# Unmasked cross attention: row maxima over pieces of 512 columns, with the last 65 columns of four tiles in one bank

## The reference, cut to what matters

```python
q = _split_heads(query @ q_w + q_b, B)      # (1, 16, 2048, 16)
k = _split_heads(key @ k_w + k_b, B)        # (1, 16, 1601, 16)
v = _split_heads(value @ v_w + v_b, B)
scores = jnp.einsum('bhqd,bhkd->bhqk', q, k) * SCALE
attn = jax.nn.softmax(scores, axis=-1)
out = jnp.einsum('bhqk,bhkd->bhqd', attn, v)
```

## Time and profile before

| | us |
|---|---|
| median of 3 executions | 3051.54 (3050.11 to 3053.46) |
| the profiled execution's own time | 3052.74 |
| its span | 3051.0 |
| busy: PE, VectorE, ScalarE, POOL | 2817.6, 2171.2, 1824.3, 542.7 |

### The profile page before, as it was taken

One profiled execution on the slowest core, in us unless ns is written; L12 is line 12 of the kernel. 1 busy time (PEld: TensorE's weight loads), 2 busy tenths in 40 slices (PEclk: granted clock), 3 DMA queues, 4 the chain that ended last, 5 costly groups with the idle time before them and its releaser, 6 DMA issues. The chain is left out here.

```text
span 3051.0 us, 93944 instructions
## 1 busy us (share of the span) xinstructions
PE 2817.6 (92%) x39186; PEld 1046.2 (34%) x39187; DVE 2171.2 (71%) x6062; ACT 1824.3 (60%) x2158; POOL 542.7 (18%) x760
## 2 busy tenths in 40 slices
PE   4999999999999999967999998999999999899997
PEld 2522222522222222233222224652222222256664
DVE  7688986587878887565899993158888888652114
ACT  2388878436666666734588886234777777831222
POOL 0188870110000000001222113111000000002330
PEclk7899999979999999978899999997999999999999
DMA  3345541301110001102111112020111111111112
GB/s 98 111 130 131 135 111 35 118 18 25 25 26 25 17 24 26 36 20 76 33 47 43 42 45 83 1 74 23 39 52 52 52 53 32 35 58 62 44 43 86
DMA packets 120407, 166.79 MB, mean 55 GB/s; under 512 B 38227, under 2 KB 89310, under 8 KB 119984
## 3 DMA queue, kind: packets, MB, share of 16 engines
q1 hardware_dynamic: 102192, 117.21, 14.3%
q0 software_dynamic: 12320, 43.02, 4.6%
q10 hardware_dynamic: 5472, 0.56, 0.2%
HBM read 126.51 MB, written 26.72 MB: 50 GB/s over the span
## 5 line engine op out<-in xcount | busy, mean ns | idle before, releaser
L737 DVE TENSOR_REDUCE mpart<-ps 128x1 f32<-128x512 f32 (+2 forms) x1792 | 1014.2, 616 | 149.2 <-PE ps L548 148.1
L548 PE MATMUL ps<-stack 48*32 48x401 f16 (+5 forms) x13312 | 987.9, 355 | 55.3 <-DVE mpart L737 25.3
L475 ACT ACTIVATE xT<-ps,exp_scale 128x1024 f32<-128x1024 f32 (+3 forms) x800 | 794.6, 1028 | 284.6 <-PE ps L569 137.5
L475 ACT ACTIVATE cn<-ps,exp_scale 128x1024 f32<-128x1024 f32 (+4 forms) x800 | 743.1, 959 | 233.6 <-PE ps L569 119.7
L569 PE MATMUL ps<-stack 50*32 50x512 f16 (+3 forms) x11648 | 744.4, 377 | 56.2 <-ACT xT L475 42.3
L548 PEld LDWEIGHTS ps<-stack 48*32 48x32 f16 x13312 | 293.3, 91 | 1056.6 <-DVE mpart L737 562.8
L733 DVE CUSTOM_DVE_ANT_0 scrap<-ps,arena 128x401 bf16<-128x401 f32 (+1 forms) x1024 | 534.3, 574 | 128.0 <-PE ps L548 128.0
L609 PE MATMUL ps<-xT,vall 128*17 128x512 f32 (+4 forms) x3648 | 422.5, 524 | 2.2 <-POOL xT L434 1.4
L609 PE MATMUL ps<-cn,vall 128*17 128x512 f32 (+3 forms) x3392 | 412.9, 508 | 1.0 <-ACT cn L475 1.0
L569 PEld LDWEIGHTS ps<-stack 50*32 50x32 f16 x11648 | 194.6, 91 | 209.2 <-ACT xT L475 110.5
L727 DVE CUSTOM_DVE_ANT_0 scrap<-ps,scrap 128x128 bf16<-128x128 f32 (+3 forms) x512 | 247.6, 485 | 19.7 <-PE ps L548 15.1
(11 more groups left out here) (281 smaller groups left out, 2510.9 us busy)
## 6 DMA issues: line engine op xcount, KB each, us to landing
stack<-q_parts SPq DMA_DIRECT2D x384, 64.0 KB, 2.6
stack<-k_parts SPq DMA_DIRECT2D x192, 64.0 KB, 2.9
wbuf<-in_maskT POOLq DMA_DIRECT2D x24, 512.0 KB, 4.7
arena<-in_moe_w SPq DMA_DIRECT2D x19, 512.0 KB, 4.4
stack<-k_parts SPq DMA_DIRECT2D x192, 50.0 KB, 2.3
stack<-sums_inverse SPq DMA_DIRECT2D x16, 512.0 KB, 5.6
parts<-osb SPq DMA_DIRECT2D x240, 32.0 KB
wbuf<-in_mask POOLq DMA_DIRECT2D x16, 401.0 KB, 4.0
```

Of the source, the lines that this page charges most:

```text
L475: nc.scalar.activation(e.prob[tile % P_SLOTS][0:rows, half * HALF + first:(half + 1) * HALF], S_PS(g)[0:rows, first:HALF], ACT.Exp, scale= ...
L548: last = nc.tensor.matmul(bank[quarter(j), 0:w], qs[b][rows, t * P + 32 * j:t * P + 32 * j + 32], ks[b][rows, a:a + w], start=True, stop=True)
L737: nc.vector.tensor_reduce(dst, src, AX, ALU.max).then_inc(unit_used, 1)
```

## The change

Where there is neither a causal nor another mask, the keys are cut in pieces of 512: three whole ones for each query tile, and the last 65 keys of four query tiles are one unit. That unit has 16 matmuls of 65 columns, which fill 260 columns of one bank, and one reduce with four results. A group of four tiles has 13 units, a head 52. The first sizes of the order follow by themselves, since it is planned from the number of units: two for each slot, and 52 + 20 = 72 in the lead-in. The least scale is 1 instead of 1/512; that touches all attentions' scales, not the instructions.

```diff
-LEAST_UP = 2.0 ** -9
+LEAST_UP = 1.0
...
     units = []
+    wide = not causal and not masked
     for t in range(NT):
         cut = tiles((t + 1) * P, CH) if causal else tiles(keys, -(-keys // -(-keys // CH)))
-        units += [(t, i, a, w, causal and a + w == (t + 1) * P) for i, (a, w) in enumerate(cut)]
+        if wide and t % 4 == 0:
+            units += [(t + j, i, a, CH, False, 1) for j in range(4) for i, (a, _) in enumerate(tiles(keys, CH)[:-1])]
+            units.append((t, keys // CH, keys // CH * CH, keys % CH, False, 4))
+        elif not wide:
+            units += [(t, i, a, w, causal and a + w == (t + 1) * P, 1) for i, (a, w) in enumerate(cut)]
...
-                    for j in range(4):
-                        last = nc.tensor.matmul(bank[quarter(j), 0:w], qs[b][rows, t * P + 32 * j:t * P + 32 * j + 32],
-                                                ks[b][rows, a:a + w], start=True, stop=True)
+                    for i in range(count):
+                        for j in range(4):
+                            at = (t + i) * P + 32 * j
+                            last = nc.tensor.matmul(bank[quarter(j), i * w:i * w + w], qs[b][rows, at:at + 32],
+                                                    ks[b][rows, a:a + w], start=True, stop=True)
                     last.then_inc(unit_ready, 1)
...
+                    elif count > 1:
+                        several = e.ps[:, g % M_BANKS, 0:count * w].rearrange("p (t n) -> p t n", n=w)
+                        nc.vector.tensor_reduce(e.mpart[h % 2][:, t:t + count, piece], several, AX, ALU.max).then_inc(unit_used, 1)
                     else:
                         nc.vector.tensor_reduce(dst, src, AX, ALU.max).then_inc(unit_used, 1)
```

More of the change, by code:

```diff
@@ L536, in unit @@
                 def unit(h, u):
-                    t, piece, a, w, diagonal = units[u]
+                    t, piece, a, w, diagonal, count = units[u]
                     g, b = h * nu + u, h % 3
```

## The result

The changed kernel takes 3002.59 us in the median of four executions (2996.10 to 3006.59) against 3052.26 us before (four as well): a ratio of 0.9835, 95% interval 0.9822 to 0.9848, so 46 to 54 us less. The forecast was 3006 us, with a range of 2986 to 3025. The profiled execution itself took 3006.59 us (span 3004.8), where the working had ended at 3007.6.

What follows compares the result with a forecast made beforehand. No engine was full; a loop set the pace: product, first unit's round trip through VectorE, and a reduce for the fifth unit. 44.7 us (heads) plus 0.4 (lead-in) off 3052.74 gave 3007.6; forecast 3006 us, range 2986 to 3025.

Steps and rivals of the forecast that it cites:

- (a): Second cross attention's loop: 52 units a head instead of 64, exactly four per cycle, so the fifth's 0.48 us goes.
- (b): Same loop: longer reduces (+0.116 us) and matmuls (+0.05, twice) make a cycle of 2.51, taken as 2.50 us.
- (c): VectorE's own pace: four wide reduces take 2.40 us, under the 2.50 cycle, so it is next bound.
- (d): 65-column unit on PE: 0.38 us, like a wide unit, no cost; as a cycle's first unit, 0.26 us less.
- serial rival: Narrow unit's 16 matmuls run one after another on PE: head 8.7 us longer, some 3190 us; chance 0.04.
- (e): Sum of a head's cycles: 33.28 us against 36.34 before, 3.06 less, over 14.6 heads 44.7 us.
- small steps: Five small steps of the maxima (L745 to L758 before the change) between one cycle's reduces: that cycle forecast at 2.71 us.
- stall: Between heads, scores wait for an exponential behind ScalarE's output copy: that cycle 3.29 us before, 3.33 forecast after.
- (f): Lead-in before the heads' loop, bound by VectorE: 42.3 us before, 41.9 after, a gain of 0.4 us.
- (g): Maxima must be in place before the next head's scores: 9.0 us needed of 9.95, slack 1 us, no cost.
- (i): PE's half-clock stretches: same number taken, 0 us, with bounds -21 (none) and +13 (one for each head).
- rival 3: More falls of PE's clock, up to one a head, as the stall idles PE longer: up to 3019 us; chance 0.15.

## Why the prediction was right

**(a), (b) The cycle.** 2.51 was worked out, 2.50 taken, 2.50 measured, with its terms 0.98, 1.19 and 0.33 at their places. The four-unit cycle of 2.29 in the trace of before was the evidence, and the run with 401 columns gives it back, as the time of most cycles.

**(c) VectorE as next bound, 0.1 us below.** Right, as far as the runs go: with the product in halves and the copy moved, a head comes within 0.4 us of VectorE's load.

**(d) The narrow unit.** Its four rounds were put 0.06 us apart, 0.38 us in all, no more than a wide unit. In the timeline of PE all sixteen matmuls take 0.30 us, and the group of them has a mean of 0.200 us from start to end, where 0.2 was taken:

```profile
2137.67 0.30 PE L555 MATMUL ps<-stack 48*32 48x65 f16 x16
```

```profile
L555 PE MATMUL ps<-stack 48*32 48x65 f16 x896 | 20.6, 200 | 1.4
```

The matmuls of the last round take 0.19 each; 0.30 less that leaves 0.11 for three steps, so the rounds are some 0.035 us apart, near the lower bound that was given. The serial rival is out. Sixteen matmuls in 0.30 us are 19 ns each, the way to the end of the last one included. The Trainium skill (TensorE: Matmul & The Clock Gate, section Back-to-back issue gap) states 81 ns for each load and matmul at 128 columns; the prediction tried that figure on 65 columns, and the trace doesn't bear it out for matmuls in four column groups. The reduce is 0.42, as worked out. So the term was taken too dear by 0.08 us: as unit A the narrow one saves 0.34 us instead of 0.26, and as the fourth it saves 0.09, where nothing was taken, since the product follows its start after 0.23 us.

**(e) The head.** Forecast 33.28, measured 33.30, but that it comes so close is luck: the parts' errors cancel. A head without half clock has nine cycles of 2.50, one of 2.41 and one of 2.16 with the narrow units, the one with the small steps and the stall of 3.32. The small steps' cycle is 2.88 instead of 2.71 (likely because VectorE nearly fills the longer cycle; not tested), the narrow ones are 0.17 below. 3.05 a head against 3.06. The 36.34 for the head before is a slip of 0.02: its cycles add up to 36.36, which is 0.3 us over the loop.

**(f) The lead-in** gained 1.5 us instead of 0.4, from 43.7 to 42.2 where the formula has 42.3 and 41.9, so most of its miss is on the kernel before. VectorE alone doesn't bound the first units, which share PE with the value projection: in the first 16 us it is busy 12.99 in the changed kernel (third number) and 14.62 before. Which wait cost the 1.1 us was not followed up.

```profile
2043.00:2059.00 16.00, 15.41 (x146) 8.40 (x144) 12.99 (x23) 3.84 (x10) 8.63 (x13) 1.00 0.34 99
```

**(g) The maxima.** From L755 to the second pair of DMAs it is 2147.23 to 2152.28, 5.05 us, where 4.5 + 0.5 was worked out; no first scores wait.

```profile
2152.28 0.54 SPq L283 DMA_DIRECT2D stack<-max_parts  x2
```

**(i) The clock.** Taken as unchanged, with -21 and +13 as bounds. In the profiled pair there are nine stretches, five of them of 3.4 us, in place of eight that were nearly all of 6.8: 44 us at half clock instead of 61. By the heads that have them against those that have none, a stretch of 6.8 us costs 2.4 us before and 2.5 to 2.6 after, one of 3.4 us costs 1.1 to 1.4, and all together they cost about 20.7 before and 16.3 after. Of these 4.4 us the first head after the lead-in and the twelfth, which is longer than its neighbours in every profile, lose about 1.5 again. What remains is 2.9 of the 3.5 us by which the loop gained more than 44.7, so this term was put at nothing and helped a little, by chance. The step that said no row tells whether shorter heads meet the stretches more often was right in that; but the stall, which rival 3 names as a cause of more falls, turned out to be where the falls are.

## What to carry to other kernels

When no engine is full, walk one period of the in-order engine's issue times and look for the operation that waits for something issued in the same period; a period that happens to have one item less prices the item for nothing. Count how many items go through the few buffers between two blocking pieces of work before widening them: here wider pieces with the same count lost 18 us, and wider pieces with fewer units gained 50. Where an engine's queue holds a copy that waits for the last piece ahead of work that is ready, try turning the two round first: here 0.8 us a head and the clock came back with it.

## What the runs showed that was not expected

The granted clock falls at the change of heads. In every profile each fall between the first scores and the last unit begins 1.7 to 4.1 us after the start of the product of a head's last key tile, in the stall or just behind it. With the stall there were 8 or 9 stretches in fifteen heads (before and after), 6 of 13.7 us with pieces of 512 unshared, 11 with two banks, 4 with the product in halves, 3 with the narrow units moved and 2 with 401 columns. With the copy moved there were 0, 0, 0 and 1. So nearly all of them come with the stall, but a stall doesn't always bring one. The length of PE's pause doesn't sort them: in the stall PE has 1.21 us without a weight load in the changed kernel, with nine falls, and 1.12 and 1.50 in the two runs with 3 and 2; in the kernel before, with eight, no gap at full clock is longer than the 0.85 us that every product has. By which rule a stall brings a fall was not found.

Executions of one kernel spread by 10 to 15 us, more than was measured at first (3050.1 to 3053.5; later 3045.6 to 3060.7 for the same kernel). The profiles show part of it in code that is the same in all of them: the second cross attention's units begin between 2038.8 and 2049.0 us. What differs there was not followed up.
